# Attention denominators by way of DRAM, both value sums in one PSUM bank, and three banks for the scores

## The chip, the cores and the metric

The kernel runs on one core of one Trainium2 chip. The metric is the device time of one execution in microseconds (us), as a median over runs. The core has five engines that work side by side and wait for each other only by semaphores: TensorE (PE in the rows; PEld is its loading of stationary operands, which runs beside the matmuls), VectorE (DVE), ScalarE (ACT), GpSimd (POOL) and SyncE (SP), which here issues nearly all DMAs. TensorE writes to PSUM, a memory of 128 partitions with eight banks of 512 fp32 columns each.

## The reference, cut to what matters

A decoder layer works on x of 4 sequences, 512 tokens and 256 channels: a Mamba block, then causal attention plus attention to a context of 1024 tokens, then a feed-forward part with eight experts. The change lies in the attention:

```python
scale = np.float32(1.0 / np.sqrt(D))            # T = 512, TC = 1024, H = 16 heads of D = 16
q, k, v = heads(x @ Wq + bq), heads(x @ Wk + bk), heads(x @ Wv + bv)
att = where(causal, einsum('bhqd,bhkd->bhqk', q, k) * scale, -inf)
y = einsum('bhqk,bhkd->bhqd', softmax(att), v)
qc, kc, vc = heads(x @ Wcq + bcq), heads(ctx @ Wck + bck), heads(ctx @ Wcv + bcv)
attc = einsum('bhqd,bhkd->bhqk', qc, kc) * scale
y = y + einsum('bhqk,bhkd->bhqd', softmax(attc), vc)
x = x + y_as_rows @ Wp + bp
```

Each softmax has its own denominator, so for each head two sums over the keys are divided by two denominators and then added.

## The kernel before

One program handles the sequences b = 0 to 3 one after the other. For each, a block holds the stages `attend(b)` (attention of sequence b), `entry(b + 1)` (the end of b's attention, its normalisation and routing, mixed with the input projections of sequence b + 1) and `scan(b + 1)` (the Mamba scan). Every stage has one program for each engine, written out by hand; an engine runs its program strictly in order and waits by semaphores. In the last block the experts follow instead of a scan.

**Attention.** The 16 heads go in NG = 4 groups g of HG = 4 heads. A group has STEPS = 12 steps k: four causal ones (k = 0 to 3, 128 keys each, against the 512, 384, 256 and 128 queries that may see them) and eight context ones (k = 4 to 11, 128 keys each against 512 queries). In a step TensorE makes for each head h a tile of scores (`scores`, bf16), keys on partitions, ScalarE takes its exponential into `probs` (L1778), GpSimd cuts the causal diagonal (`masks`, L1498), and TensorE adds values times probabilities to the sums (`values(g, k)`, fp32, four heads side by side in 32 rows each). `values` of step k - 1 stands behind the scores of step k. The values have a column of ones, so row HD = 16 of each head's 32 rows holds its denominator.

**PSUM.** Banks 0 to 3 are two slots for the maxima, 4 and 5 the ring of score tiles (tile n waits until tile n - 2 is read), 6 holds the context sums, 7 the causal ones. The softmax subtracts true maxima: while group g is worked on, TensorE also makes the scores of group g + 1 as 24 jobs (`max_job`; 8 causal, 16 context, two matmuls or more each) and VectorE reduces them (L1813, L1809). The maxima are turned (`max_rows_out`, L1604), split into bf16 parts on VectorE (`negated_parts`, L1825 to L1830) and loaded by SyncE. `JOBS_AT` says how many jobs stand in each step: two per step while groups 1 and 2 are worked on, none in group 3, a mixed list in group 0. In a step with two jobs the order on TensorE is scores of heads 0 and 1, a job, scores of heads 2 and 3, a job, values; jobs that must wait for a turn stand behind the values.

**Denominators.** ScalarE copies bank 7 into `Y2` behind step 9 (L1761) and bank 6 into `Y1` behind the next group's step 0 (L1753). In the next group's step 1 TensorE spreads the denominator rows over all 128 partitions with a matmul by the 0-1 matrix `den_sel` (`denominators`, two fp32 matmuls of 512 columns in two ring slots), ScalarE copies the two results (L1767), and GpSimd and VectorE form (Y1 * d2 + Y2 * d1) / (d1 * d2): product on GpSimd (L1526), reciprocal on VectorE (L1835, or L1158 for group 3), three more multiplications and an addition on GpSimd, the last of them (L1536) into `YT[g]`. For group 3 this tail lies between the last attention step and `project`, the product with Wp, in `entry`: there TensorE first turns the next sequence's rows (`to_columns`), makes half of its input projection and then `project`; in the last block `project` follows at once.

## Time and profile before

| what | us |
|---|---|
| time, median of 3 runs (1931.35 to 1934.1) | 1931.47 |
| the profiled execution | 1937.27 |
| its span, first to last instruction | 1935.5 |
| TensorE busy in it | 1519.7 (79%) |
| VectorE busy | 1356.8 (70%) |
| ScalarE busy | 852.4 (44%) |
| GpSimd busy | 716.3 (37%) |
| mean DMA rate | 76 GB/s |
| TensorE's line L166 (nearly all matmuls), share of the chain that ended last | 16% |

The granted TensorE clock has a mean of 0.917 of full speed. Busy shares are means over stages of different kinds: in the scan VectorE is the busiest, in the attention TensorE. So they say little by themselves, and the stages have to be read one by one. The four attentions are alike: the copies of the context sums stand at 294.0, 335.4, 376.7 and 409.2 us for b = 0, and the same distances (41.3 to 41.4, 41.3 to 41.4 and 32.5 us) return for b = 1, 2 and 3. "L166" is a helper that records almost every matmul, so those are told apart by their tiles.

### The profile page before, as it was taken

How to read it: one execution, taken by the hardware profiler on the slowest of the kernel's cores; microseconds unless marked ns; L12 is line 12 of the kernel's file. 1: busy time of each engine (PE TensorE's matmuls, PEld its weight loads, DVE VectorE, ACT ScalarE, POOL GpSimd, SP SyncE). 2: the span in 40 equal slices, each digit the busy share in tenths (PEclk: the TensorE clock that was granted, in tenths of full speed). 3: DMA queues.
4: the chain of work that ended last, by engine and by line, in shares of the span. 5: the costliest groups of instructions: out<-in, count | busy, mean ns of one | idle time of the engine just before them, and what ended most of it. 6: DMA issues, size and time to landing. Idle time of an engine off the chain costs nothing. (4 is left out here: it accounts for less than half of the span.)

```text
span 1935.5 us, 19324 instructions
## 1 busy us (share of the span) xinstructions
PE 1519.7 (79%) x6456; PEld 726.0 (38%) x6456; DVE 1356.8 (70%) x2009; ACT 852.4 (44%) x1618; POOL 716.3 (37%) x678
## 2 busy tenths in 40 slices
PE   5697789883987798884977888845677998669995
PEld 2354322231554222142544222322232221458874
DVE  5998587658995777479995876579977684434334
ACT  3543346654543356644433466544333567212211
POOL 2564332322864412226653322227644222222221
PEclk9799889996999799987999799978998899779998
DMA  4930441003002530012004420021014300247754
GB/s 134 341 105 24 112 91 42 1 1 118 20 1 70 137 62 1 1 51 85 3 1 120 107 42 2 1 88 45 1 40 125 73 10 1 66 129 247 239 171 132
DMA packets 123843, 147.17 MB, mean 76 GB/s; under 512 B 18725, under 2 KB 106542, under 8 KB 121696
## 3 DMA queue, kind: packets, MB, share of 16 engines
q1 hardware_dynamic: 120000, 137.27, 24.4%
q0 software_dynamic: 3744, 8.66, 1.2%
q8 instruction: 51, 0.84, 0.2%
q14 instruction: 48, 0.39, 0.1%
HBM read 96.53 MB, written 50.79 MB: 76 GB/s over the span
## 5 line engine op out<-in xcount | busy, mean ns | idle before, releaser
L166 PE MATMUL PS<-arena 128*32 128x512 f32 (+10 forms) x4150 | 862.8, 451 | 117.6 <-ACT arena L1778 30.1
L166 PEld LDWEIGHTS PS<-arena 128*32 128x32 f32 (+3 forms) x4150 | 363.9, 128 | 598.3 <-ACT arena L1778 269.7
L1778 ACT ACTIVATE arena<-PS 128x512 f32<-128x512 f32 (+3 forms) x768 | 375.3, 541 | 271.0 <-PE PS L166 269.1
L1353 POOL TENSOR_TENSOR arena<-arena 128x1024 f32<-128x1024 f32 x128 | 305.1, 2385 | 239.1 <-DVE arena L1379 139.8
L1809 DVE TENSOR_REDUCE maxs<-PS 128x1 f32<-128x1024 f32 x256 | 301.3, 1216 | 53.6 <-PE PS L166 53.3
L1379 DVE TENSOR_TENSOR_SCAN arena<-PS,arena 128x1024 f32<-128x1024 f32 x128 | 292.1, 2282 | 6.1 <-ACT PS L1328 6.1
L1328 ACT ACTIVATE PS<-arena,A_neg 128x511 f32<-128x511 f32 x256 | 165.9, 681 | 240.3 <-DVE arena L1379 191.0
L166 PE MATMUL PS<-arena,ident 128*128 128x512 f32 (+1 forms) x560 | 259.8, 590 | 5.4 <-DVE arena L1388 5.4
L1498 POOL TENSOR_SCALAR_AFFINE_SELECT arena<-arena 128x128 f32<-128x128 f32 x256 | 73.7, 300 | 324.4 <-ACT arena L1778 320.4
L1388 DVE TENSOR_TENSOR arena<-arena,PS 128x1024 f32<-128x1024 f32 x128 | 156.2, 1220 | 6.9 <-PE PS L166 2.8
L1813 DVE TENSOR_REDUCE maxs<-PS 128x1 f32<-128x512 f32 (+3 forms) x256 | 107.9, 481 | 62.8 <-PE PS L166 62.0
L166 PE MATMUL PS<-bc,bc_sel 96*128 96x512 bf16 x128 | 52.1, 407 | 121.0 <-DVE arena L1388 114.4
L166 PEld LDWEIGHTS PS<-arena,ident 128*128 128x128 f32 x560 | 109.4, 199 | 91.9 <-issue 74.5
L530 POOL DMA_INDIRECT picked_rows<-arena x46 | 45.3, 985 | 142.7 <-DVE arena L708 82.7
L166 PEld LDWEIGHTS PS<-bc,bc_sel 96*128 96x128 bf16 x128 | 12.5, 97 | 174.6 <-DVE arena L1388 163.6
L1487 POOL TENSOR_TENSOR arena<-arena 128x512 bf16<-128x512 f32 x40 | 46.0, 1155 | 81.2 <-ACT arena L1724 81.2
L1801 DVE SCALAR_TENSOR_TENSOR arena<-PS,bqk,arena 128x512 f32<-128x512 f32 x40 | 29.5, 747 | 63.9 <-ACT arena L1719 63.9
L1719 ACT ACTIVATE arena<-PS,bqk 128x512 bf16<-128x512 f32 x40 | 26.9, 683 | 94.5 <-PEq L173 52.7
L617 ACT ACTIVATE arena<-PS,arena 128x256 f32<-128x256 f32 x60 | 25.2, 471 | 91.7 <-PE PS L166 91.7
L1526 POOL TENSOR_TENSOR arena<-xn 128x512 f32<-128x512 f32 x16 | 20.3, 1266 | 114.9 <-ACT xn L1767 114.9
L166 PE MATMUL PS<-xT,in_w 128*128 128x512 f32 x128 | 59.3, 619 | 3.1 <-DVE xT L1154 3.1
L1835 DVE RECIPROCAL arena<-arena 128x512 f32<-128x512 f32 x12 | 40.1, 3344 | 28.7 <-POOL arena L1526 28.7
(260 smaller groups left out, 1632.1 us busy)
## 6 DMA issues: line engine op xcount, KB each, us to landing
arena<-in_ew SPq DMA_DIRECT2D x46, 512.0 KB, 4.6
arena<-stack_parts SPq DMA_DIRECT2D x288, 64.0 KB, 2.2
rows_in<-nil SPq DMA_DIRECT2D x16, 1088.0 KB, 12.5
arena<-b_rows SPq DMA_DIRECT2D x16, 1024.0 KB, 7.6
stack_parts<-arena SPq DMA_DIRECT2D x40, 384.0 KB, 2.5
arena<-stack_parts SPq DMA_DIRECT2D x96, 128.0 KB, 4.1
arena<-rows_in SPq DMA_DIRECT2D x23, 272.0 KB, 5.0
arena<-picked_rows SPq DMA_DIRECT2D x16, 256.0 KB, 3.5
```

The costliest lines, as they stand in the source:

```text
L166: return nc.tensor.matmul(o, l, r, start=start, stop=stop)
L530: nc.gpsimd.indirect_dma_start(picked_rows, bass.IndirectOffsetOnAxis(ap=row_id[i % NIB][:, r:r + 1].bitcast(I32), axis=0), eo[i % NEB][:, ...
L1328: last = nc.scalar.activation(decay(i)[:, k, 1:T], delta[:, 2 * kh + k, 1:T], ACT.Exp, scale=A_neg[:, 2 * kh + k, n:n + 1])
L1353: nc.gpsimd.tensor_tensor(b_sb[i % 2], u[:, 2 * kh:2 * kh + 2, :], Brow[:, n, :].unsqueeze(1).to_broadcast([P, 2, T]), ALU.mult).then_inc( ...
L1379: nc.vector.tensor_tensor_scan(h_sb[i % 2].rearrange(flat), decay(i).rearrange(flat), b_sb[i % 2].rearrange(flat), 0.0, ALU.mult, ALU.add)\
L1388: nc.vector.tensor_tensor(g_sb[i % 2], h_sb[i % 2], bank(6).unsqueeze(1).to_broadcast([P, 2, T]), ALU.mult).then_inc(S["g_done"], 1)
L1487: nc.gpsimd.tensor_tensor(pt[i % NPT][:, 2, :], r_sb[i % 2], pt[i % NPT][:, 1, :], ALU.subtract)\
L1498: nc.gpsimd.affine_select(out=own, in_=own, compare_op=ALU.is_ge, fill=0.0, base=0, pattern=[[1, P]], channel_multiplier=-1).then_inc(S["m ...
L1778: nc.scalar.activation(probs[(HG * s + h) % NPR][:, 0:N], bank(4 + n % 2)[:, 0:N], ACT.Exp, scale=HD ** -0.5).then_inc(S["ring_read"], 1)
L1809: last = nc.vector.reduce_max(maxs[:, g % 2, CONTEXT, h * TT + r:h * TT + r + 1], PS[:, 2 * s:2 * s + 2, :].rearrange("p a n -> p (a n)"), ...
L1813: last = nc.vector.reduce_max(maxs[:, g % 2, CAUSAL, h * TT + q:h * TT + q + 1], bank(2 * s + c_)[:, 0:(q + 1) * P], AXX)
L1835: nc.vector.reciprocal(R2, R1).then_inc(S["norm_ready"], 1)
```

## The change

The tail of each group is done in another way, and the PSUM banks are given out anew.

- Both sums of a group use bank 6, causal first, then context. `copy_causal` moves from behind step 9 to behind step 4, and `values` of step 0 and step 4 wait for the copy of the sum before them. Bank 7 joins the ring of score tiles, which has three banks now.
- `Y1`, `Y2` become two pairs of buffers `YS`, taken in turn by the groups.
- For groups 0 to 2 the `den_sel` matmuls, ScalarE's copies of them, and the reciprocal of 128x512 are gone. SyncE gathers the denominator rows into `den_c` (32 partitions of 128), VectorE inverts that in place, SyncE writes it to `dens` in DRAM and reads it back, each head's row repeated over 32 partitions, into `den_sb`. GpSimd then does two multiplications and an addition. SyncE's loads of group 3's heads, of 24 DMAs, stand between the gather and the write for group 0; the loads of the rows of maxima for group g + 2 stand behind the read.
- For group 3 TensorE multiplies the sums, as stationary operand, with four columns of `den_sel` (`turned_sums`: eight fp32 matmuls of 4 columns), VectorE inverts 32 columns and repeats each 32 times (`last_sums`), TensorE turns that into two banks (`spread_sums`: eight fp32 matmuls of 128 columns), and VectorE multiplies and adds (`last_heads`).

ScalarE's order around the end of group 1. L1761 and L1753 (before), L1799 and L1791 (after) are the copies of the causal and the context sums, L1767 the copies of the spread denominators, L1778 and L1809 the exponentials. Before:

```order
L1778 ACTIVATE arena<-PS 128x512 x24
L1761 ACTIVATE arena<-PS 128x512
L1778 ACTIVATE arena<-PS 128x512 x12
L1753 ACTIVATE arena<-PS 128x512
L1778 ACTIVATE arena<-PS 128x384 x4
L1767 ACTIVATE xn<-PS 128x512 x2
L1778 ACTIVATE arena<-PS 128x256 x4
```

After:

```order
L1809 ACTIVATE arena<-PS 128x512 x4
L1799 ACTIVATE arena<-PS 128x512
L1809 ACTIVATE arena<-PS 128x512 x32
L1791 ACTIVATE arena<-PS 128x512
L1809 ACTIVATE arena<-PS 128x384 x4
L1809 ACTIVATE arena<-PS 128x256 x4
```

The causal copy moved from behind 24 context exponentials to behind four; the two denominator copies are gone.

TensorE's order from the last values of group 3 on (`32x512` is a head's part of `values`), before:

```order
L166 MATMUL PS<-arena 32x512 x8
L166 MATMUL PS<-arena,den_sel 128x512 x2
L452 MATMUL PS<-ident,arena 128x128 x8
L166 MATMUL PS<-xT,in_w 128x512 x8
L166 MATMUL PS<-wp,arena 128x256 x16
```

After:

```order
L170 MATMUL PS<-arena 32x512 x8
L170 MATMUL PS<-den_sel,arena 128x4 x8
L456 MATMUL PS<-ident,arena 128x128 x8
L170 MATMUL PS<-ident,xn 128x128 x8
L170 MATMUL PS<-xT,in_w 128x512 x8
L170 MATMUL PS<-wp,arena 128x256 x16
```

Sixteen matmuls in two places stand where two stood; the second eight are ahead of the input projection.

VectorE's order at the same place (the first row of each is its copy in the turning of x, the last the convolution), before:

```order
L1154 COPY xT<-PS 128x512
L1155 MEMSET arena 128x4x3
L1158 RECIPROCAL arena<-arena 128x512
L1053 TENSOR_SCALAR arena<-arena,conv_w,conv_b 128x512
L1056 SCALAR_TENSOR_TENSOR arena<-arena,conv_w 128x512 x3
```

After:

```order
L1173 RECIPROCAL den_t<-PS 128x32
L1175 COPY xn<-den_t 128x1024
L1193 COPY xT<-PS 128x512
L1194 MEMSET arena 128x4x3
L1182 TENSOR_TENSOR arena<-arena,PS 128x512
L1183 TENSOR_TENSOR arena<-arena,PS 128x512
L1184 TENSOR_TENSOR arena<-arena 128x512
L1074 TENSOR_SCALAR arena<-arena,conv_w,conv_b 128x512
```

A short reciprocal and a copy now stand ahead of the copy of x, and three multiplications and additions take the place of the long reciprocal.

The diff, cut to its core:

```diff
@@ -50,6 +50,7 @@
...
     picked_rows = nc.dram_tensor("picked_rows", (NOWHERE, DM), F32).ap()
+    dens = nc.dram_tensor("dens", (2, HG, T), F32).ap()
@@ -125,6 +126,9 @@
...
         mrest = sb("mrest", [HG * TT, P])
+        den_c = sb("den_c", [2 * HG * TT, P])
+        den_t = sb("den_t", [P, 2 * TT * HG])
+        den_wide = xn[:].rearrange("p (i a) n -> p i (a n)", i=2)
@@ -355,7 +359,7 @@
...
         yt_end = used[0]
-        Y1, Y2, R1, R2 = ar(T), ar(T), ar(T), ar(T)
+        YS = [(ar(T), ar(T)) for _ in range(2)]
@@ -756,10 +760,7 @@
...
         def ring(g, k, h):
-            return HG * (STEPS * g + k) + h + 2 * max(g - 1, 0) + (2 if g >= 1 and k >= 2 else 0)
-
-        def ring_den(g, i):
-            return HG * STEPS * (g + 1) + 2 * g + i + (2 * HG if g + 1 < NG else 0)
+            return HG * (STEPS * g + k) + h
@@ -827,6 +828,22 @@
...
             def tensor(pe):
+                def turned_sums():
+                    pe.wait_ge(S["pv_copied"], 2 * NG)
+                    for i, y in enumerate(YS[(NG - 1) % 2]):
+                        for t in range(TT):
+                            last = mm(bank(5)[:, (i * TT + t) * HG:(i * TT + t + 1) * HG], y[:, tok(t)],
+                                      den_sel[:, 0:P:32], i + t == 0, i + t == TT)
+                    last.then_inc(S["turned_mm"], 1)
+
+                def spread_sums():
+                    pe.wait_ge(S["den_ready"], NG)
+                    for i in range(2):
+                        for t in range(TT):
+                            last = mm(bank(6 + i)[:, tok(t)], den_wide[:, i, tok(t)],
+                                      ident[:], True, True)
+                    last.then_inc(S["turned_mm"], 1)
+
@@ -889,7 +906,11 @@
...

+                if ends:
+                    pe.wait_ge(S["ring_read"], HG * STEPS * NG)
+                    turned_sums()
                 if not begins:
+                    spread_sums()
@@ -898,9 +919,9 @@
...
                     to_columns(pe, xnE, TT * ends, 0)
+                    if ends:
+                        spread_sums()
                     pe.wait_ge(S["xT_ready"], 2 + 2 * ends)
-                    if ends:
-                        pe.wait_ge(S["ring_read"], ring_den(NG - 1, 1) + 1)
@@ -1147,15 +1168,32 @@
...

+                def last_sums():
+                    dve.wait_ge(S["turned_mm"], 1)
+                    fed(nc.vector.reciprocal(den_t[:], bank(5)[:, 0:2 * TT * HG]))
+                    dve.wait_ge(S["y_ready"], NG - 1)
+                    nc.vector.tensor_copy(den_wide.rearrange("p i (c n) -> p (i c) n", n=32),
+                                          den_t[:].unsqueeze(2).to_broadcast([P, 2 * TT * HG, 32]))\
+                        .then_inc(S["den_ready"], 1)
+
+                def last_heads():
+                    dve.wait_ge(S["turned_mm"], 2)
+                    y = YS[(NG - 1) % 2]
+                    fed(nc.vector.tensor_tensor(y[0], y[0], bank(6), ALU.mult))
+                    fed(nc.vector.tensor_tensor(y[1], y[1], bank(7), ALU.mult))
+                    nc.vector.tensor_tensor(YT[NG - 1], y[0], y[1], ALU.add).then_inc(S["y_ready"], 1)
+
...
                     normalise(dve, link, x_sb, xnE)
+                if ends:
+                    last_sums()
+                if begins:
...
                 if ends:
-                    dve.wait_ge(S["den_ready"], NG)
-                    nc.vector.reciprocal(R2, R1).then_inc(S["norm_ready"], 1)
+                    last_heads()
@@ -1393,6 +1431,11 @@
...
             CAUSAL, CONTEXT = 0, 1
+            RING = (4, 5, 7)
+
+            def ring_bank(n):
+                return bank(RING[n % len(RING)])
+
@@ -1469,12 +1512,24 @@
...
                 load_max_rows(1, CONTEXT)
-                sp.wait_ge(S["pv_mm"], STEPS)
-                for x in range(4):
-                    load_heads(3, x)
-                for g in range(2, NG):
-                    for side in range(2):
-                        load_max_rows(g, side)
+                for g in range(NG - 1):
+                    sp.wait_ge(S["pv_copied"], 2 * (g + 1))
+                    for i, y in enumerate(YS[g % 2]):
+                        sp.dma_start(den_c[i * HG * TT:(i + 1) * HG * TT, :], y[HD:P:32, :])\
+                            .then_inc(S["dens_out"], 16)
+                    if g == 0:
+                        for x in range(4):
+                            load_heads(3, x)
+                    sp.wait_ge(S["den_ready"], g + 1)
+                    sp.dma_start(dens.rearrange("i h (q p) -> (i h q) p", p=P), den_c[:]).then_inc(S["dens_kept"], 16)
+                    sp.wait_ge(S["dens_kept"], 16 * (g + 1))
+                    sp.wait_ge(S["y_ready"], g)
+                    for i in range(2):
+                        sp.dma_start(den_sb[:, i, :], dens[i].unsqueeze(1).to_broadcast([HG, 32, T]))\
+                            .then_inc(S["dens_in"], 16)
+                    if g + 2 < NG:
+                        load_max_rows(g + 2, CAUSAL)
+                        load_max_rows(g + 2, CONTEXT)
@@ -1518,22 +1573,14 @@
...
                 pool.wait_ge(S["ones_ready"], 2 * NPAR)
-                for g in range(NG):
-                    if g + 1 < NG:
-                        masks(g + 1, 0)
-                        masks(g + 1, 1)
-                    pool.wait_ge(S["ring_read"], ring_den(g, 1) + 1)
-                    nc.gpsimd.tensor_tensor(R1, den_sb[:, 0, :], den_sb[:, 1, :], ALU.mult)\
-                        .then_inc(S["den_ready"], 1)
-                    if g + 1 < NG:
-                        masks(g + 1, 2)
-                    nc.gpsimd.tensor_tensor(Y1, Y1, den_sb[:, 1, :], ALU.mult)
-                    if g + 1 < NG:
-                        masks(g + 1, 3)
-                    link(nc.gpsimd.tensor_tensor(Y2, Y2, den_sb[:, 0, :], ALU.mult))
-                    link(nc.gpsimd.tensor_tensor(Y1, Y1, Y2, ALU.add))
-                    pool.wait_ge(S["norm_ready"], g + 1)
-                    nc.gpsimd.tensor_tensor(YT[g], Y1, R2, ALU.mult).then_inc(S["y_ready"], 1)
+                for g in range(NG - 1):
+                    for k in range(TT):
+                        masks(g + 1, k)
+                    pool.wait_ge(S["dens_in"], 2 * 16 * (g + 1))
+                    y = YS[g % 2]
+                    nc.gpsimd.tensor_tensor(y[0], y[0], den_sb[:, 0, :], ALU.mult)
+                    link(nc.gpsimd.tensor_tensor(y[1], y[1], den_sb[:, 1, :], ALU.mult))
+                    nc.gpsimd.tensor_tensor(YT[g], y[0], y[1], ALU.add).then_inc(S["y_ready"], 1)
@@ -1608,9 +1655,9 @@
...
                         n = ring(g, k, h)
-                        if n >= 2:
-                            pe.wait_ge(S["ring_read"], n - 1)
-                        o = bank(4 + n % 2)
+                        if n >= len(RING):
+                            pe.wait_ge(S["ring_read"], n - len(RING) + 1)
+                        o = ring_bank(n)
@@ -1618,21 +1665,15 @@
...

-                def denominators(g):
-                    pe.wait_ge(S["pv_copied"], 2 * (g + 1))
-                    for i, y in enumerate((Y1, Y2)):
-                        pe.wait_ge(S["ring_read"], ring_den(g, i) - 1)
-                        mm(bank(4 + ring_den(g, i) % 2), den_sel[:], y, True, True).then_inc(S["ring_mm"], 1)
-
...
                     if k == 0 and g >= 1:
-                        pe.wait_ge(S["pv_copied"], 2 * g - 1)
-                    if k == TT and g >= 1:
                         pe.wait_ge(S["pv_copied"], 2 * g)
+                    if k == TT:
+                        pe.wait_ge(S["pv_copied"], 2 * g + 1)
@@ -1640,7 +1681,7 @@
...
                         else:
-                            last = mm(bank(7)[rows, k * P:T], V[:, k, HG * g + h, :],
+                            last = mm(bank(6)[rows, k * P:T], V[:, k, HG * g + h, :],
@@ -1698,8 +1739,6 @@
...
                             max_job(g + 1, i)
-                        if k == 1 and g >= 1:
-                            denominators(g - 1)
@@ -1750,22 +1788,15 @@
...
                     act.wait_ge(S["pv_mm"], STEPS * (g + 1))
-                    nc.scalar.activation(Y1, bank(6), ACT.Copy).then_inc(S["pv_copied"], 1)
+                    nc.scalar.activation(YS[g % 2][0], bank(6), ACT.Copy).then_inc(S["pv_copied"], 1)
...
                         all_stored(act)
-                    else:
-                        act.wait_ge(S["y_ready"], g)
+                    if g >= 2:
+                        act.wait_ge(S["y_ready"], g - 1)
                     act.wait_ge(S["pv_mm"], STEPS * g + TT)
-                    nc.scalar.activation(Y2, bank(7), ACT.Copy).then_inc(S["pv_copied"], 1)
-
-                def copy_denominators(g):
-                    for i in range(2):
-                        n = ring_den(g, i)
-                        act.wait_ge(S["ring_mm"], n + 1)
-                        nc.scalar.activation(den_sb[:, i, :], bank(4 + n % 2), ACT.Copy)\
-                            .then_inc(S["ring_read"], 1)
+                    nc.scalar.activation(YS[g % 2][1], bank(6), ACT.Copy).then_inc(S["pv_copied"], 1)
@@ -1775,16 +1806,13 @@
...
                         act.wait_ge(S["ring_mm"], n + 1)
-                        nc.scalar.activation(probs[(HG * s + h) % NPR][:, 0:N], bank(4 + n % 2)[:, 0:N], ACT.Exp,
+                        nc.scalar.activation(probs[(HG * s + h) % NPR][:, 0:N], ring_bank(n)[:, 0:N], ACT.Exp,
...
                         copy_context(g - 1)
-                    if g >= 1 and k == 1:
-                        copy_denominators(g - 1)
-                    if k == STEPS - 3:
+                    if k == TT:
...
                 copy_context(NG - 1)
-                copy_denominators(NG - 1)
@@ -1831,8 +1859,10 @@
...
                 def invert(g):
-                    dve.wait_ge(S["den_ready"], g + 1)
-                    nc.vector.reciprocal(R2, R1).then_inc(S["norm_ready"], 1)
+                    dve.wait_ge(S["dens_out"], 2 * 16 * (g + 1))
+                    if g:
+                        dve.wait_ge(S["dens_kept"], 16 * g)
+                    nc.vector.reciprocal(den_c[:], den_c[:]).then_inc(S["den_ready"], 1)
@@ -1858,11 +1888,10 @@
...
                         negated_parts(g + 1, CAUSAL)
-                        maxima(g + 1, range(KJOBS, KJOBS + 4))
...
                     if g + 1 < NG:
-                        maxima(g + 1, range(KJOBS + 4, JOBS))
+                        maxima(g + 1, range(KJOBS, JOBS))
...
                     for k in range(KM):
```

## Rows read from the trace of the kernel before

**Rows 1.** Stretches (us): busy PE, PEld, DVE, ACT, POOL; granted clock; DMA share, GB/s.
```profile
294.00:335.36 41.36, 37.35 (x215) 11.04 (x214) 31.91 (x41) 25.73 (x52) 10.78 (x21) 1.00 0.22 49
376.71:409.18 32.47, 25.73 (x144) 5.98 (x142) 10.14 (x26) 23.44 (x48) 9.48 (x17) 1.00 0.01 1
```
**Rows 2.** Timeline of ScalarE: start, duration, instruction, idle time before and its releaser.
```profile
291.43 2.17 ACT L1778 ACTIVATE arena<-PS 128x512 f32<-128x512 f32 x4 [1.22 <-PE PS L166]
...
304.64 2.17 ACT L1778 ACTIVATE arena<-PS 128x512 f32<-128x512 f32 x4 [1.07 <-PE PS L166]
...
322.63 2.17 ACT L1778 ACTIVATE arena<-PS 128x512 f32<-128x512 f32 x4 [1.21 <-PE PS L166]
...
326.01 2.17 ACT L1778 ACTIVATE arena<-PS 128x512 f32<-128x512 f32 x4 [0.72 <-PE PS L166]
```
**Rows 3.** Timeline of TensorE's weight loads, one context step with two maxima jobs.
```profile
318.76 0.55 PEld L166 LDWEIGHTS PS<-arena 99*128 99x128 bf16 x4 [0.84 <-ACT arena L1778]
319.90 0.10 PEld L166 LDWEIGHTS PS<-arena 99*128 99x128 bf16 x1 [0.59 <-ACT arena L1778]
320.39 0.33 PEld L166 LDWEIGHTS PS<-arena 99*128 99x128 bf16 x3 [0.39 <-ACT arena L1778]
```
**Rows 4.** Timeline of VectorE in the same group, behind the turn of the maxima.
```profile
307.10 4.62 DVE L1809 TENSOR_REDUCE maxs<-PS 128x1 f32<-128x1024 f32 x4
311.63 3.34 DVE L1835 RECIPROCAL arena<-arena 128x512 f32<-128x512 f32 x1
```
**Rows 5.** Timeline, a context step of group 3: ScalarE and TensorE's weight loads.
```profile
402.79 2.16 ACT L1778 ACTIVATE arena<-PS 128x512 f32<-128x512 f32 x4 [0.29 <-PE PS L166]
403.44 0.10 PEld L166 LDWEIGHTS PS<-arena 99*128 99x128 bf16 x1 [1.02 <-ACT arena L1778]
...
403.93 0.10 PEld L166 LDWEIGHTS PS<-arena 99*128 99x128 bf16 x1 [0.39 <-ACT arena L1778]
...
405.24 0.11 PEld L166 LDWEIGHTS PS<-arena 99*128 99x128 bf16 x2 [0.84 <-ACT arena L1778]
```
**Rows 6.** Timeline, the end of the attention of b = 0.
```profile
409.18 0.60 ACT L1753 ACTIVATE arena<-PS 128x512 f32<-128x512 f32 x1 [1.29 <-PE PS L166]
...
409.83 1.98 PE L166 MATMUL PS<-arena,den_sel 128*128 128x512 f32 x4 [0.72 <-ACT arena L1753]
...
413.47 7.13 PE L166 MATMUL PS<-xT,in_w 128*128 128x512 f32 x16 [0.78 <-DVE xT L1154]
...
417.17 0.70 DVE L1053 TENSOR_SCALAR arena<-arena,conv_w,conv_b 128x512 f32<-128x512 f32 x1
```
**Rows 7.** Timeline, the same place for b = 3.
```profile
1650.10 0.60 ACT L1753 ACTIVATE arena<-PS 128x512 f32<-128x512 f32 x1 [1.29 <-PE PS L166]
...
1659.88 9.56 PE L166 MATMUL PS<-wp,arena 128*128 128x256 f32 x32 [7.15 <-POOL arena L1536]
```
**Rows 8.** Timeline of TensorE in the scan.
```profile
103.72 0.38 PE L166 MATMUL PS<-bc,bc_sel 96*128 96x512 bf16 x1
103.94 2.32 PE L166 MATMUL PS<-arena,ident 128*128 128x512 f32 x8
106.10 1.24 PE L166 MATMUL PS<-arena 128*128 128x256 f32 x5
```
**Rows 9.** Groups of instructions by form: busy us, mean ns of one, idle before.
```profile
L1388 DVE TENSOR_TENSOR arena<-arena,PS 128x1024 f32<-128x1024 f32 x128 | 156.2, 1220 | 6.9 <-PE PS L166 2.8
...
L1526 POOL TENSOR_TENSOR arena<-xn 128x512 f32<-128x512 f32 x16 | 20.3, 1266 | 114.9 <-ACT xn L1767 114.9
L1146 DVE TENSOR_TENSOR arena<-arena 128x512 f32<-128x512 f32 x16 | 19.5, 1218 | 1.9 <-ACT arena L988 1.9
```
**Rows 10.** DMA issues on the page: count, KB each, median us to landing.
```profile
arena<-stack_parts SPq DMA_DIRECT2D x288, 64.0 KB, 2.2
...
arena<-b_rows SPq DMA_DIRECT2D x16, 1024.0 KB, 7.6
```
**Rows 11.** Timeline of SyncE: its queue issues the loads of group 3's heads.
```profile
294.70 11.56 SPq L1430 DMA_DIRECT2D arena<-stack_parts  x24
```

5 lines of the change are left out of this document (2 added, 3 removed).

## The prediction

> **What bounds the kernel now.** I read three views: busy time by stretch, to see which engine fills a group of the attention; the timelines of single steps there, to see what TensorE waits for; and the timeline of the attention's end, where the change adds a serial chain. A group of the middle (from one context copy to the next) takes 41.36 us with TensorE busy for 37.35, VectorE for 31.91 and ScalarE for 25.73; group 3, with no maxima to make, takes 32.47 us with TensorE at 25.73 and ScalarE at 23.44 [rows 1]. So no engine is full, and TensorE is the nearest to it. The bracket [0.59 <-ACT] in the steady context step tells what it lacks: the load for head 2's scores stands at 319.90 until ScalarE has freed a bank, that for head 3 at 320.39 until it has freed the next [rows 3]. Group 3 repeats it: 403.44 and 403.93, each after an exponential [rows 5]. With two banks, TensorE's order ties it to ScalarE twice in every step. ScalarE itself is not full: four exponentials take 2.17 us, and it then stands still for 1.21 us until TensorE is through with job, values and next score [rows 2]. The bound is this round trip, and the scores' ring sets it.
>
> **The third bank.** Head 2's scores now need the bank that head 3 of the step before used, free for long. Head 3's need head 0's bank, the release on which head 2 waited before. So head 3, and all behind it, moves from 320.39 to 319.90, by 0.49 us; in group 3 from 403.93 to 403.44, again 0.49 [rows 3, 5]. Does TensorE get there in time? From 318.76 it has two scores, a job of two matmuls and head 2's scores ahead of head 3's, five bf16 matmuls of 512 columns at 0.22 us (103.72 to 103.94) [rows 8]: 1.10 us, to 319.86. It just fits. ScalarE's 2.17 us fit into the new step of 3.38 - 0.49 = 2.89 us (322.63 to 326.01 is 3.38 now) [rows 2], and so do two maxima of 4.62 / 4 = 1.16 us [rows 4]. Where it applies the gain is 0.49 us a step:
> - Groups 1 and 2, eight context steps each. Behind the turn VectorE is late, so one or two steps stay longer, but the reciprocal of 3.34 us between the maxima [rows 4] becomes one of 128 columns, 3.34 / 4 = 0.84 us, ahead of them. I take 4.0 us a group, about 8 x 0.49.
> - The four causal steps have tiles of 512 down to 128 columns and exponentials to match, so the gain shrinks with them; I take 1.1 us a group.
> - Group 0: its first steps hold three or four jobs and are paced by VectorE; the last four gain 2.0 us.
> - Group 3: 8 x 0.49 = 3.9 us and 1.1 for the causal steps, less 0.9 below.
>
> **Denominators of groups 0 to 2.** TensorE loses two fp32 products of 512 columns, four passes. Four passes and four of 128 columns take 106.10 - 103.94 = 2.16 us; at a rate by columns that is 0.43 and 0.11 us each [rows 8], so 1.72 us go. It also waited there for ScalarE, as at the end of group 3 (0.72) [rows 6]; I take 2.0 us in all, and the first four steps, 13.21 us long (291.43 to 304.64) [rows 2], get shorter by 3.1. Five GpSimd operations of 1.27 us [rows 9] become three. GpSimd has 10.78 us of work in a group of 41.36 [rows 1], so that gives nothing.
>
> What comes in is a chain by way of SyncE. From the copy in step 0: a gather, a reciprocal, a write, a read of two times 256 KB, three GpSimd operations. 64 KB land in 2.2 us, and one of four loads of 1024 KB in 7.6 us [rows 10], so the small transfers are 2 us each and the read 2 to 8 us. Behind the first gather SyncE issues 24 loads in 11.56 us [rows 11]; the write queues behind them. Worst: 0.6 + 2 + 11.6 + 2 + 8 + 3.8 = 28 us, and the new group has about 34; the buffers that it frees are wanted only a group later. Queued behind SyncE's waits are the rows of maxima for group g + 2, wanted 34 us after they are made. VectorE waits for the gather at step 4, some 10 us into the group, when it has landed. All hidden, cost 0.
>
> **One bank for both sums.** `values` of step 0 wait for the context copy, `values` of step 4 for the causal one. Both stand behind a whole step's scores, and head 3's scores themselves need an exponential that ScalarE makes after the copy. So the copy is done when `values` ask, and its price is its 0.6 us on ScalarE, where that is short. In steps of 2.89 us with 2.17 of exponentials it is hidden (before, too, it cut the idle time from 1.21 to 0.72) [rows 2]. In group 3 a step is 2.94 - 0.49 = 2.45 us against 2.16 [rows 5]: 0.3 shows. There step 4, behind the short step 3, is also paced by ScalarE and does not gain its 0.49. I take 0.9 together; the bounds are 0 and, if a copy lay bare, 0.6 + 2.17 = 2.8 us for each of 32 copies.
>
> **Sum of an attention.** Groups 1 and 2: 4.0 + 3.1 = 7.1 each. Group 3: 3.9 + 3.1 - 0.9 = 6.1. Group 0: 2.0. Together 22.3 us; times four, 89.2.
>
> **The end, b = 0 to 2.** Time runs from ScalarE's copy at 409.18 [rows 6]. Now the input projection begins at 4.29. After: the copy ends at 0.6; `turned_sums` are 16 passes of 4 columns behind fp32 weight loads. The trace has no such pass: nearest is the fp32 pass of 128 columns at 0.11 [rows 8]; below it is some 0.03, above a 128-column load and a pass one after the other, 0.3. I take 0.09, 1.5 us, to 2.2. VectorE's reciprocal of 32 columns is 3.34 / 16 = 0.2 [rows 4], its copy of 1024 columns 0.6 to 1.2 (1.22 for a product of that size) [rows 9]: to 3.9 with semaphores. The turning of x, and its copies, lie beside. `spread_sums` are 16 passes of 128 columns, 1.8 us, to 5.7. The projection begins 1.4 us later than now, and `project` with it. VectorE's two products from PSUM (half of 1.22 each) and one sum in SBUF (1.22) [rows 9] end near 8.3, against 8.0 when the convolution starts now [rows 6], and the long reciprocal and its wait are gone. So + 1.4 us, three times + 4.2. Bounds: 0.5 and, with 0.3 us for all 32 passes, 6.5 each.
>
> **The end, b = 3.** Now `project` begins 1659.88 - 1650.10 = 9.78 us after the copy [rows 7]. After: 8.3, so - 1.5. TensorE stood still for 7.15 us, and `project` then took 9.56 us for 32 passes of 256 columns, where 0.22 each would be 6.9. With shorter gaps some of that may come back. I take - 2 in all (0 to - 4).
>
> **Sum.** - 89.2 + 4.2 - 2 = - 87 us. The profiled execution took 1937.27 us, with 1.8 outside its span; it becomes 1850.3. The median of the runs lies 5.8 below the profiled one: 1844.5, so 1845.
>
> **A rule that speaks against it.** In the read back from DRAM each of four heads' rows is repeated 32 times, and the outer dimension of the source is 4. The trace shows no such read; its load of repeated rows has the partitions outermost and lands in 7.6 us for 1024 KB [rows 10]. The Trainium skill, DMA: Bandwidth & Descriptors, Rules for kernel authors, says that an outer dimension below 16 confines a DMA to so many of the 16 engines, and names a leading broadcast as the case. By that rule the two reads would share four engines; the sum would be the same as long as rival 2's condition is not met.
>
> **The rivals.**
> 1. *VectorE takes the place of the ring.* It has 31.91 us of work in a group [rows 1], less 2.5 for the reciprocal, and the new group has 34. Its maxima follow TensorE's jobs through two slots, so a late one stops TensorE, and the catching up behind the turn may take four steps and not two. For it: after the turn VectorE runs 4.62 and 3.34 us without a gap [rows 4]. Against: per step 2.3 us against 2.89. Then about half of the gain of 28 steps x 4 is lost, 0.25 x 112 = 28 us: 1873.
> 2. *The DRAM chain is late.* If the read runs at a quarter of the rate, 256 KB take 4 x 256 / 1024 x 5.6 = 5.6 us beyond the fixed 2, two of them 13 us. In group 3 the chain of group 2 is then 3.2 + 0.6 + 2 + 0.9 + 2 + 13 + 3.8 = 25.5 us, against 26 for the group and 3 more until VectorE needs it: hidden. It decides from 29 us on; at twice the read it costs 9 us in each attention: 1880. This is the skill's rule above, taken to one or two engines.
> 3. *The waits on ScalarE are not what they seem.* If each step is held by something that the brackets do not name, only the den_sel matmuls go: 3 x 2 x 4 = 24 us, + 2 at the ends: 1910.
> 4. *Slower: the shared bank lays the copies bare.* If each handover of bank 6 stops TensorE, that is 32 times up to 2.8 us, 90 us; it decides from 87 / 32 = 2.7 us a handover. Against: a step's scores stand between. It would give 1845 + 90 = 1935.
>
> **Chances.** The forecast, 1830 to 1865: 0.62. Rival 1: 0.16. Rival 2: 0.06. Rival 3: 0.06. Rival 4: 0.03, with ends of 6.5 us each and less gain in the ring. Faster than 1830: 0.07. Range 1830 to 1882, which holds the forecast, rival 1 mostly and rival 2. About 0.2% (4 us) is what a measurement of this kernel can tell from no change. Faster by more: 0.95; within: 0.02; slower: 0.03.
>
> **What would show it.** In the changed profile: context steps of 2.9 us in groups 1 and 2 and 2.45 in group 3, with one wait for ScalarE per step instead of two; middle groups of 34 us, group 3 near 26; the projection starting about 5.7 us after the last copy. Rival 1 would show VectorE without gaps and TensorE waiting for L1837; rival 2 VectorE's copy waiting for GpSimd; rival 4 `values` waiting for ScalarE's copies. The prediction fails first if the steps do not shrink by 0.49 us.

## The result, and the profile after the change

The changed kernel takes 1850.99 us (median of 4 runs, 1846.17 to 1856.06) beside 1932.78 us for the kernel before (4 runs, 1931.35 to 1935.59): a ratio of 0.9575, 95% interval 0.9544 to 0.9607. The prediction of 1845 us with a range of 1830 to 1882 held. The profiled execution took 1853.68 us, where the prediction's own sum had 1850.3. Timed once more in a later set the ratio was 0.957 [0.9546, 0.9594].

Two stretches by busy time, the first from one context copy to the next, the second group 3 (columns: length, then busy time with the number of instructions for PE, PEld, DVE, ACT and POOL, then granted clock, DMA share, GB/s). They answer to [rows 1]:

```profile
289.56:323.99 34.43, 33.11 (x211) 10.19 (x210) 28.22 (x41) 23.62 (x50) 8.25 (x19) 1.00 0.33 75
358.42:384.85 26.43, 22.23 (x140) 5.18 (x138) 6.00 (x26) 21.13 (x46) 7.38 (x16) 1.00 0.07 23
```

A middle group is 6.9 us shorter, group 3 is 6.0 us shorter, and TensorE now works for 33.1 of 34.4 us in a middle group, where it worked for 37.35 of 41.36. The same lengths return in all four attentions (one middle group of b = 2 is 34.71 us long). What a step looks like now, in ScalarE's timeline (start, duration, instruction, idle time before and its releaser), first groups 1 and 2, then group 3; they answer to [rows 2, 5]:

```profile
304.54 2.06 ACT L1809 ACTIVATE arena<-PS 128x512 f32<-128x512 f32 x4 [1.20 <-PE PS L170]
307.43 2.07 ACT L1809 ACTIVATE arena<-PS 128x512 f32<-128x512 f32 x4 [0.83 <-PE PS L170]
...
364.41 2.06 ACT L1809 ACTIVATE arena<-PS 128x512 f32<-128x512 f32 x4 [0.67 <-PE PS L170]
366.34 0.63 ACT L1799 ACTIVATE arena<-PS 128x512 f32<-128x512 f32 x1
366.81 2.12 ACT L1809 ACTIVATE arena<-PS 128x512 f32<-128x512 f32 x4
369.32 2.06 ACT L1809 ACTIVATE arena<-PS 128x512 f32<-128x512 f32 x4 [0.39 <-PE PS L170]
371.77 2.07 ACT L1809 ACTIVATE arena<-PS 128x512 f32<-128x512 f32 x4 [0.39 <-PE PS L170]
```

The steps are 307.43 - 304.54 = 2.89 us and 371.77 - 369.32 = 2.45 us. The weight loads of the same step show what is left of TensorE's waits, to be read against [rows 3]:

```profile
306.94 0.76 PEld L170 LDWEIGHTS PS<-arena 99*128 99x128 bf16 x5 [0.84 <-ACT arena L1809]
308.08 0.33 PEld L170 LDWEIGHTS PS<-arena 99*128 99x128 bf16 x3 [0.38 <-ACT arena L1809]
```

The scores of heads 0 and 1, the job and the scores of head 2 run through (five loads in one row), and the next load waits for ScalarE; before, head 2 and head 3 each waited.

The end of the attention of b = 0, TensorE and VectorE, to be read against [rows 6] (the passes of fp32 count twice, as x16):

```profile
385.59 1.92 PE L170 MATMUL PS<-den_sel,arena 128*128 128x4 f32 x16 [0.81 <-ACT arena L1791]
387.37 1.07 PE L456 MATMUL PS<-ident,arena 128*128 128x128 f32 x8
388.69 2.05 PE L170 MATMUL PS<-ident,xn 128*128 128x128 f32 x16 [0.25 <-DVE xn L1175]
390.58 3.60 PE L170 MATMUL PS<-xT,in_w 128*128 128x512 f32 x8
...
387.55 0.36 DVE L1173 RECIPROCAL den_t<-PS 128x32 f32<-128x32 f32 x1 [18.89 <-PE PS L170]
387.94 0.69 DVE L1175 COPY xn<-den_t 128x1024 f32<-128x1024 f32 x1
```

The projection begins 390.58 - 384.85 = 5.73 us behind the last copy (4.29 before). The same row of `spread_sums` is longer behind b = 1 (3.35 us) and b = 2 (3.65 us), and the stretch around it has a lower granted clock; here is b = 1, and the stretch behind b = 0 and 1:

```profile
778.32 3.35 PE L170 MATMUL PS<-ident,xn 128*128 128x128 f32 x16 [0.25 <-DVE xn L1175]
```

```profile
386.90:390.60 3.70, 3.45 (x31) 3.21 (x31) 1.67 (x4) 0.60 (x1) 0.00 (x0) 1.00 0.00 0
776.90:781.40 4.50, 4.25 (x27) 4.02 (x27) 1.67 (x4) 0.60 (x1) 0.00 (x0) 0.71 0.00 0
```

Last, the chain through DRAM, in SyncE's and GpSimd's timelines of the first middle group:

```profile
290.87 1.25 SPq L1518 DMA_DIRECT2D den_c<-arena  x2
292.17 11.46 SPq L1473 DMA_DIRECT2D arena<-stack_parts  x24
303.67 0.42 SPq L1524 DMA_DIRECT2D dens<-den_c  x1
308.91 1.16 SPq L1528 DMA_DIRECT2D xn<-dens  x2
...
316.81 1.27 POOL L1581 TENSOR_TENSOR arena<-arena,xn 128x512 f32<-128x512 f32 x1 [19.64 <-DMA xn<-dens]
...
319.38 1.27 POOL L1583 TENSOR_TENSOR arena<-arena 128x512 f32<-128x512 f32 x1
322.56 0.29 POOL L1553 TENSOR_SCALAR_AFFINE_SELECT arena<-arena 128x128 f32<-128x128 f32 x1 [1.90 <-ACT arena L1809]
```

GpSimd's third operation ends at 320.65, 31.1 us behind the copy at 289.56. The row below it is the first mask of the next group, which GpSimd takes up 1.90 us later. That bracket is all the slack that the chain has on GpSimd here.

Where the 83.6 us of the two profiled executions came from (us over all four sequences). "Tiles" are ScalarE's first reads of the query and key projections ahead of the attention (L1719 before, L1757 after); the other cuts are its copies of the context sums:

| stretch | predicted | measured |
|---|---|---|
| start of the program to the first tile of b = 0 | 0 | -1.1 |
| last tile to the first copy: group 0, with step 0 of group 1 | -8.0 | -14.0 |
| groups 1 and 2 | -56.8 | -55.0 |
| group 3 | -24.4 | -24.2 |
| last copy to the next block's first tile (the end and the scan), b = 0 to 2 | +4.2 | +7.4 |
| first to last tile | 0 | +2.6 |
| behind the last attention | -2.0 | +0.75 |
| sum | -87.0 | -83.6 |

### The profile page after: what moved, and what is told of

Same layout as the page of the kernel before. It is cut to its first block and busy times, and to the rows that moved or that the text cites. A ratio compares the mean times of both kernels' runs of the same rounds, so it can differ in the third digit from the quotient of the medians.

```text
span 1851.9 us, 19445 instructions
## 1 busy us (share of the span) xinstructions
PE 1474.7 (80%) x6520; PEld 730.4 (39%) x6520; DVE 1306.0 (71%) x2025; ACT 818.5 (44%) x1586; POOL 660.6 (36%) x634
## 5 line engine op out<-in xcount | busy, mean ns | idle before, releaser
L170 PE MATMUL PS<-arena 128*32 128x512 f32 (+10 forms) x4150 | 830.2, 449 | 84.4 <-DVE maxs L1837 22.0
L1809 ACT ACTIVATE arena<-PS 128x512 f32<-128x512 f32 (+3 forms) x768 | 361.6, 549 | 225.5 <-PE PS L170 224.4
L1581 POOL TENSOR_TENSOR arena<-arena,xn 128x512 f32<-128x512 f32 x12 | 15.3, 1274 | 163.1 <-DMA xn<-dens 163.1
L1757 ACT ACTIVATE arena<-PS,bqk 128x512 bf16<-128x512 f32 x40 | 26.9, 682 | 97.4 <-PEq L177 52.8
L646 DVE CAST arena<-arena 128x2 int32<-128x2 f32 x23 | 4.1, 176 | 78.3 <-PE PS L547 68.9
```

The lines of the kernel that those rows point to most:

```text
L170: return nc.tensor.matmul(o, l, r, start=start, stop=stop)
L1809: nc.scalar.activation(probs[(HG * s + h) % NPR][:, 0:N], ring_bank(n)[:, 0:N], ACT.Exp, scale=HD ** -0.5).then_inc(S["ring_read"], 1)
```

## Experiments

All edits are to the changed kernel. "Middle group" is the distance between the context copies of groups 0 and 1, and of 1 and 2.

**1. The third bank, taken away.**

```diff
-            RING = (4, 5, 7)
+            RING = (4, 5)
```

> The changed kernel with a ring of two banks (4 and 5); bank 7 lies idle, everything else is as changed. Theory (the third bank carries most of the gain, 0.49 us a step): context steps back at 3.38 us in groups 1 and 2 and at 2.94 in group 3; middle groups of about 38.6 to 39.3 us (34.43 with three banks), group 3 of about 31 (26.43); 17 us more per attention, about 1920 us in all, which would leave some 13 us of the 82 to the denominators alone. Rival (the two waits on ScalarE in each step are not what holds it; only the den_sel matmuls that went did): middle groups stay within 1 us of 34.4 and the time within 10 us of 1851.

Measured: 1918.65 us (4 runs), ratio to the kernel before 0.9929 [0.9901, 0.9957]. Middle groups of 38.38 us, group 3 of 31.78 us (b = 0 and 3), 30.70 (b = 1) and 30.47 (b = 2). The difference within group 3 goes with the granted clock, b = 0 first, then b = 1:

```profile
370.51:402.29 31.78, 25.29 (x140) 5.37 (x138) 6.11 (x26) 22.25 (x46) 7.16 (x15) 0.95 0.06 19
778.25:808.95 30.70, 23.77 (x140) 5.30 (x138) 6.20 (x26) 22.25 (x46) 7.15 (x15) 1.00 0.06 19
```

TensorE's weight loads in a context step:

```profile
308.72 0.55 PEld L170 LDWEIGHTS PS<-arena 99*128 99x128 bf16 x4 [0.84 <-ACT arena L1809]
309.86 0.10 PEld L170 LDWEIGHTS PS<-arena 99*128 99x128 bf16 x1 [0.59 <-ACT arena L1809]
310.35 0.33 PEld L170 LDWEIGHTS PS<-arena 99*128 99x128 bf16 x3 [0.39 <-ACT arena L1809]
```

Both waits of [rows 3] are back, 0.49 us apart (309.86, 310.35), and the step is 3.38 us again. So the ring carries 1918.65 - 1850.99 = 67.7 of the 82 us; the prediction's terms for it are 5.1 + 5.1 + 5.0 + 2.0 = 17.2 in each attention, 69 in all. Rival 3 falls.

**2. Banks of their own for the two sums, with a ring of two.** It differs from experiment 1 in the sharing alone.

```diff
-            RING = (4, 5, 7)
+            RING = (4, 5)
...
-                    if k == 0 and g >= 1:
-                        pe.wait_ge(S["pv_copied"], 2 * g)
-                    if k == TT:
-                        pe.wait_ge(S["pv_copied"], 2 * g + 1)
+                    if k == 0 and g >= 1:
+                        pe.wait_ge(S["pv_copied"], 2 * g - 1)
+                    if k == TT and g >= 1:
+                        pe.wait_ge(S["pv_copied"], 2 * g)
...
-                            last = mm(bank(6)[rows, k * P:T], V[:, k, HG * g + h, :],
+                            last = mm(bank(7)[rows, k * P:T], V[:, k, HG * g + h, :],
...
-                    nc.scalar.activation(YS[g % 2][1], bank(6), ACT.Copy).then_inc(S["pv_copied"], 1)
+                    nc.scalar.activation(YS[g % 2][1], bank(7), ACT.Copy).then_inc(S["pv_copied"], 1)
```

> A ring of two banks again, and bank 7 now takes the causal sums, so that causal and context sums have banks of their own as in the kernel before; `values` wait for the copy of a group earlier. It differs from the run with two banks in the sharing alone, and from the kernel before in the way of the denominators alone. Theory (the handover of the shared bank is hidden behind a step's scores): the same time as the run with two banks within 4 us, about 1920. Rival (each of the 32 handovers stops TensorE by 0.3 us or more): at least 10 us faster than the run with two banks. Against the kernel before, the theory gives what the denominators' way saves by itself: 3 x 3.1 us less 0.5 x 3 per attention at most, 5 to 20 us in all.

Measured: 1921.08 us (5 runs), ratio 0.993 [0.9904, 0.9956]. Middle groups of 38.38 us, the same to the hundredth as with the shared bank; group 3 of 31.79 at b = 0 and 31.78 at b = 3, as in experiment 1. At b = 1 and 2 it is 31.95 and 33.29 us long, 1.25 and 2.8 us longer than there, at a granted clock of 0.95 and 0.85 where experiment 1 has 1.00; so banks of their own are nowhere faster. The handovers cost nothing that can be measured, with two banks in the ring. With three, in group 3, where ScalarE is short, the two steps around the causal copy take 369.32 - 364.41 = 4.91 us, twice the 2.45 of a step without it. Rival 4 falls.

The two runs also split a middle group: 41.34 to 38.38 by the other way of the denominators (2.96 us), 38.38 to 34.43 by the ring (3.95 us). The whole kernel shows less of the first part: experiments 1 and 2 are 12 to 15 us faster than the kernel before, where 8 x 2.96 is 23.7. The stretches between the attentions, which hold the changed ends, took back 10 us of it (the first two rows of the table under experiment 8).

**3. The chain through DRAM, left out.**

```diff
...
-                    for i, y in enumerate(YS[g % 2]):
-                        sp.dma_start(den_c[i * HG * TT:(i + 1) * HG * TT, :], y[HD:P:32, :])\
-                            .then_inc(S["dens_out"], 16)
...
-                    sp.wait_ge(S["den_ready"], g + 1)
-                    sp.dma_start(dens.rearrange("i h (q p) -> (i h q) p", p=P), den_c[:]).then_inc(S["dens_kept"], 16)
...
-                    if g >= 1:
-                        invert(g - 1)
...
-                    pool.wait_ge(S["dens_in"], 2 * 16 * (g + 1))
+                    pool.wait_ge(S["pv_copied"], 2 * (g + 1))
```

> The changed kernel without the chain through DRAM in groups 0 to 2: the gather, VectorE's inversion, the write and the read are left out (30 DMAs and 3 reciprocals of 0.93 us per attention), and GpSimd multiplies by whatever lies in den_sb as soon as the sums are copied. The denominators of these groups are therefore not computed; the last group's are. Theory (chain fully hidden): the same time within 4 us, 1851; at most the standstill of 1 us behind the turn in the middle groups shrinks by VectorE's 0.93 us, 8 times, so a gain of 0 to 7 us. Rival (the chain delays TensorE through SyncE's queue, DMA traffic or GpSimd's masks): faster by more than 10 us.

Measured: 1862.5 us (4 runs), ratio 0.9626 [0.9597, 0.9655]: work was left out and the kernel became 11.5 us slower. Neither theory had that sign. Middle groups of 35.35 and 36.82 us. VectorE behind the turn in the second, and GpSimd at the same time:

```profile
336.04 0.84 DVE L1847 CAST mparts<-mrest 16x128 bf16<-16x128 f32 x1
336.92 1.38 DVE L1848 TENSOR_TENSOR mparts<-mrest,mparts 16x128 bf16<-16x128 f32 x1
338.23 4.69 DVE L1827 TENSOR_REDUCE maxs<-PS 128x1 f32<-128x1024 f32 x4
...
335.54 1.27 POOL L1572 TENSOR_TENSOR arena<-arena,xn 128x512 f32<-128x512 f32 x1
336.89 1.26 POOL L1573 TENSOR_TENSOR arena<-arena 128x512 f32<-128x512 f32 x1
```

VectorE's two operations end at 336.88 and 338.30, each just behind the end of one of GpSimd's (336.81, 338.15). In the changed kernel the same two take 0.21 and 0.28 us, because the chain holds GpSimd's work back until 316.81. The maxima behind them start when GpSimd is through. That such reads of PSUM are not held up is seen in the changed kernel, where two of them take 2.36 us, their usual 1.2 us each, beside the operation of GpSimd at 316.81:

```profile
316.70 2.36 DVE L1837 TENSOR_REDUCE maxs<-PS 128x1 f32<-128x1024 f32 x2 [0.54 <-PE PS L170]
```

The 1.73 us lost, less the 0.93 us of the inversion that is gone, are 0.8 of the 0.92 us by which the first middle group is longer; in the second TensorE's clock fell as well (0.95 over the group), behind 2.26 us in which it waited for the maxima. Over the four attentions the groups are 13.3 us longer by the trace.

**4. The same, with GpSimd's work held back.**

```diff
                     pool.wait_ge(S["pv_copied"], 2 * (g + 1))
+                    pool.wait_ge(S["ring_read"], HG * (STEPS * (g + 1) + 10))
```

> As the run without the chain through DRAM (the denominators of groups 0 to 2 are not computed, their gather, inversion, write and read left out), but GpSimd's three operations on a group's sums wait until the tenth step of the next group, when the changed kernel has them too (316 us). In the run without the chain they began right behind the masks, at 334.3, while VectorE's CAST and TENSOR_TENSOR on mparts took 0.84 and 1.38 us (0.21 and 0.28 in the changed kernel). Theory (GpSimd's SBUF work and VectorE's SBUF-to-SBUF work hold each other up, and that made the run without the chain 11 us slower): those two are back at 0.21 and 0.28 us, middle groups are 33.5 to 34.4 us long, and the time is 1842 to 1851. Rival (the chain's absence shifts something else, such as the loads of maxima): middle groups stay at 35.3 and 36.8 us, the time near 1862.

Measured: 1851.99 us (4 runs), ratio 0.9574 [0.9554, 0.9594]; middle groups of 34.03 us. GpSimd's first operation begins at 316.00, and VectorE's two rows are back:

```profile
299.83 0.21 DVE L1848 CAST mparts<-mrest 16x128 bf16<-16x128 f32 x1
300.08 0.28 DVE L1849 TENSOR_TENSOR mparts<-mrest,mparts 16x128 bf16<-16x128 f32 x1
```

One wait more, and the kernel is 10.5 us faster; by the traces the eight middle groups together are 289.02 us long in experiment 3 and 272.55 here. So it was the meeting of the two engines, and what followed from it. The chain itself (DMAs, SyncE's queue, the inversion of 0.93 us) costs 34.43 - 34.03 = 0.4 us in a middle group and no more.

**5. The chain made longer: the read made four times, and twice.**

```diff
-                    for i in range(2):
-                        sp.dma_start(den_sb[:, i, :], dens[i].unsqueeze(1).to_broadcast([HG, 32, T]))\
-                            .then_inc(S["dens_in"], 16)
+                    for r in range(4):
+                        for i in range(2):
+                            sp.dma_start(den_sb[:, i, :], dens[i].unsqueeze(1).to_broadcast([HG, 32, T]))\
+                                .then_inc(S["dens_in"], 16)
+                        sp.wait_ge(S["dens_in"], 2 * 16 * (4 * g + r + 1))
```

> The changed kernel with the read back from DRAM made four times, each pair of DMAs waited for by SyncE before the next is issued: the read takes about 4 x 7.9 = 32 us instead of 7.9, so the chain is some 24 us longer. Theory (the chain ends 8.3 us before group 3 does: 376.5 against 384.85, and GpSimd's product is wanted by VectorE's copy 3 us behind that, so 11 us of slack): the end of the attention, between the last copy and the input projection, becomes 12 to 15 us longer, 4 x 13 = 52 us, and more where the middle groups' masks and buffers are late too; the time is 1895 to 1960. Rival (the slack is larger than read, GpSimd's work being wanted only later): less than 10 us more in all.

Measured with four reads: 2056.87 us (4 runs), 206 us more and not 52. By stretches at b = 0: the first middle group 57.04 us (+22.6), the second 50.20 (+15.8), group 3 26.43 (unchanged), and VectorE's copy at the end came 14.99 us behind the last context copy in place of 3.09 (+11.9). Only this last term had been expected with a number. For the others I took GpSimd's queue: the masks of the next group stand behind its three operations, and `values` of step 0 wait for the masks. The slack on that path was read off the changed trace, and the read made twice (the same edit with 2 for 4) was to put it to the test:

> The changed kernel with the read back from DRAM made twice, so that the chain is some 8 us longer. With the read made four times the chain was 23 us longer, and the groups between context copies became 22.6 and 15.8 us longer and the end 11.9. Theory (the chain is wanted first where the next group's masks queue behind GpSimd's three operations; its slack in the changed trace is 322.56 - 320.65 = 1.9 us in the first middle group, 356.99 - 347.87 = 9.1 in the second, and 387.94 - 376.50 = 11.4 at the end): the first middle group becomes 6 to 8 us longer, 40.5 to 42.5 us, the second stays at 34.4 to 35.5, group 3 at 26.4, the end unchanged; 24 to 32 us in all, 1875 to 1883. Rival (the chain is wanted only at the end of a group or later, as the prediction took it): all groups unchanged, 1851.

Measured: 1886.46 us (one time). The first middle group is 42.64, 42.37, 41.69 and 42.14 us long, the second 34.42 (34.70 at b = 2, as unchanged), group 3 27.64 for b = 0 to 2 and 26.44 for b = 3. Columns as in the first fence:

```profile
291.66:334.30 42.64, 34.42 (x211) 10.44 (x210) 28.31 (x41) 23.70 (x51) 8.54 (x20) 0.92 0.30 73
334.30:368.72 34.42, 33.11 (x211) 10.18 (x210) 28.21 (x41) 23.72 (x51) 7.98 (x18) 1.00 0.09 33
368.72:396.36 27.64, 23.73 (x140) 5.28 (x138) 6.01 (x26) 21.17 (x47) 7.38 (x16) 0.94 0.12 41
```

The middle groups are about as long as expected, but another wait ended last. In the first middle group SyncE, GpSimd and TensorE's weight loads have:

```profile
327.46 7.36 SPq L1481 DMA_DIRECT2D arena<-mparts  x6
...
330.08 1.26 POOL L1585 TENSOR_TENSOR arena<-arena 128x512 f32<-128x512 f32 x1
...
330.49 0.14 PEld L170 LDWEIGHTS PS<-arena 99*128 99x128 bf16 x2 [7.83 <-issue]
...
331.87 0.29 POOL L1555 TENSOR_SCALAR_AFFINE_SELECT arena<-arena 128x128 f32<-128x128 f32 x1 [0.53 <-ACT arena L1811]
```

TensorE stands still for 7.83 us ahead of the first scores of group 2, not ahead of `values`. It goes on at 330.49, before GpSimd's third operation ends (331.34), and the first mask then waits for ScalarE. What the scores of step 0 wait for in the program is the rows of maxima of their group. SyncE loads these behind the read, and the edit also makes it wait until the last read has landed. TensorE goes on 3.03 us behind the first of these loads (327.46); with four reads it is 3.02 and 3.08 us (339.32 to 342.34, and 389.47 to 392.55). In the second middle group of this run the loads begin at 361.23 and the scores are due at 366.12: nothing is lost. So the edit's cost in the middle groups came by way of SyncE's queue. GpSimd's way would have cost nearly as much: its third operation ends 39.68 us behind the context copy in place of 31.09, 8.6 us later for a slack of 1.9. That slack is read from the changed trace; no run tests it by itself. In the changed kernel the same loads begin at 310.11, and the scores of group 2 at 321.40, so that way has some 8 us of slack.

Group 3 is 1.2 us longer for b = 0 to 2 at a granted clock of 0.94, which the expectation did not have; that is 3.6 of the 35 us, where 24 to 32 had been expected in all.

**6. The read with 32 repeats outermost.**

```diff
-                        sp.dma_start(den_sb[:, i, :], dens[i].unsqueeze(1).to_broadcast([HG, 32, T]))\
-                            .then_inc(S["dens_in"], 16)
+                        for h in range(HG):
+                            sp.dma_start(den_sb[32 * h:32 * h + 32, i, :], dens[i, h].partition_broadcast(32))\
+                                .then_inc(S["dens_in"], 16)
```

> The read back from DRAM as eight DMAs of one head each, whose outermost dimension is 32 repeats, in place of two with an outermost dimension of 4. In the changed kernel the two moved at some 100 GB/s with a DMA share of 0.20 to 0.25, and GpSimd began 7.9 us after the first was issued. Rival (the rate is set by the DRAM side or the packets of 2 KB, whatever the order): rate and share as before, GpSimd 8 us or more behind. In either case the time is within 5 us of 1851, since the chain is hidden.

Measured: 1847.63 us (one time; nothing follows from it alone). GpSimd begins 314.95 - 309.80 = 5.15 us behind the first issue in place of 316.81 - 308.91 = 7.90. A stretch in the middle of the read, first of the changed kernel, then of this one (the last two columns are DMA share and GB/s):

```profile
311.00:316.00 5.00, 5.00 (x30) 1.33 (x30) 4.46 (x4) 3.45 (x7) 0.00 (x0) 1.00 0.27 100
```

```profile
311.00:315.00 4.00, 4.00 (x22) 1.15 (x22) 2.93 (x4) 2.78 (x6) 0.05 (x1) 1.00 0.40 127
```

A share of 0.27 is 4.3 of 16 engines, with the small loads of the maxima among it. The Trainium skill's rule that the prediction weighed (DMA: Bandwidth & Descriptors, Rules for kernel authors: an outer dimension of 4 keeps a DMA on 4 of the 16 engines) agrees with it. With eight DMAs the share is 0.40, below the 0.5 expected, and SyncE takes 3.56 us to issue them; that issuing now sets the pace is likely, but was not tried. What the two DMAs cost is 2.75 us of a chain that lies hidden: middle groups are 34.42 us long with eight DMAs too.

**7. `turned_sums` with passes of 128 columns.**

```diff
-                            last = mm(bank(5)[:, (i * TT + t) * HG:(i * TT + t + 1) * HG], y[:, tok(t)],
-                                      den_sel[:, 0:P:32], i + t == 0, i + t == TT)
+                            last = mm(bank(4 + i)[:, tok(t)], y[:, tok(t)], den_sel[:], True, True)
...
-                    fed(nc.vector.reciprocal(den_t[:], bank(5)[:, 0:2 * TT * HG]))
+                    fed(nc.vector.reciprocal(den_t[:].rearrange("p (i c) -> p i c", i=2), PS[:, 4:6, 0:T:32]))
```

> `turned_sums` stream all 128 columns of den_sel (8 fp32 products of 128 columns, into banks 4 and 5) in place of 4 of them, and VectorE's reciprocal reads every 32nd column of the result; all else is as changed. In the changed kernel the granted clock over `spread_sums` was 1.00 behind b = 0, but 0.60 and 0.54 behind b = 1 and 2, where they took 3.3 us in place of 2.0. Theory (the passes of 4 columns count as rest for the clock): with the wide ones `spread_sums` are granted 1.00 behind every b, take 2.0 us, and the projection begins 5.8 us behind the last copy in all of them, so 2.6 us less in all, or nothing measurable but visible in the trace. Rival (the clock falls from the standstill while VectorE inverts and copies, or from what lies ahead): the clock over `spread_sums` stays below 0.7 in b = 1 and 2.

Measured: 1844.67 us (4 runs), ratio 0.9542 [0.9523, 0.9562], which overlaps the changed kernel's interval. The mean of 0.71 behind b = 1 lies between the two levels of the clock, half (1.2 GHz) and full (2.4 GHz). The same stretch here, and the rows in it:

```profile
776.30:780.10 3.80, 3.50 (x31) 3.26 (x31) 1.67 (x4) 0.60 (x1) 0.00 (x0) 1.00 0.00 0
```

```profile
775.04 2.02 PE L170 MATMUL PS<-den_sel,arena 128*128 128x128 f32 x16 [0.81 <-ACT arena L1790]
...
778.24 2.05 PE L170 MATMUL PS<-ident,xn 128*128 128x128 f32 x16 [0.30 <-DVE xn L1174]
```

Thirty-two times the columns cost 2.02 us in place of 1.92, the clock stays at 1.00 there behind b = 1 and 2, and `spread_sums` take 2.05 us behind all four, so 1.3, 1.6 and 0.8 us less behind b = 1, 2 and 3. The other traces bear this out behind b = 3 alone: there `spread_sums` take 2.8 to 3.8 us in all ten with passes of 4 columns, and 2.05 us in all three with 128. Behind b = 0 to 2 the narrow passes alone do not explain the clock: experiments 3 and 6 have them too, and take 2.05 us each time, as experiment 7 does. So what lies ahead of them counts as well, and the gain there is not shown to be the wide passes' doing. Nor is it shown that the whole kernel is faster by them.

**8. The ends in another order** (the turning of x ahead of `turned_sums`, two products of the projection ahead of `spread_sums`, the first convolution ahead of `last_heads`).

```diff
                     to_columns(pe, xnE, TT * ends, 0)
                     if ends:
-                        spread_sums()
+                        pe.wait_ge(S["ring_read"], HG * STEPS * NG)
+                        turned_sums()
                     pe.wait_ge(S["xT_ready"], 2 + 2 * ends)
                     for m in range(2 * DT):
+                        if ends and m == 2:
+                            spread_sums()
...
                 if ends:
-                    last_heads()
+                    last_sums()
                 if begins:
                     conv(0)
+                if ends:
+                    last_heads()
```

> The changed kernel with the ends b = 0 to 2 in another order: the turning of x and its copy stand ahead of `turned_sums`, two products of the input projection (m = 0, 1) ahead of `spread_sums`, and VectorE makes the first convolution ahead of the last group's products. Theory (the projection waits for the serial chain of the last denominators only because it stands behind it): it begins 2 to 4.3 us behind the last copy in place of 5.73, and the ends get shorter by 1.3 to 2.9 us each: 4 to 9 us in all, 1842 to 1847. Rival (the end is set by VectorE's work on the heads and by `project`, whatever stands ahead of it): within 3 us of 1851.

Measured: 1849.47 us (5 runs), ratio 0.9566 [0.9549, 0.9582]: within 2 us of the changed kernel. That is the rival's time but not its reason, since the end itself did as meant:

```profile
386.60:397.00 10.40, 10.40 (x55) 7.05 (x54) 6.83 (x12) 2.98 (x5) 0.00 (x0) 1.00 0.01 2
```

```profile
389.12 3.68 PE L170 MATMUL PS<-xT,in_w 128*128 128x512 f32 x8
```

TensorE works without a gap, and the projection begins 2.52 us behind the last copy. `project` begins 11.26 us behind it for b = 0 to 2, in place of 12.60, 14.24 and 14.23, so the three ends are 7.3 us shorter. At the next attention 3.3 us are left of that. Lengths from the last context copy of b to the first of b + 1:

| version | b = 0 | b = 1 | b = 2 |
|---|---|---|---|
| before | 296.23 | 301.21 | 297.99 |
| 1, two banks | 299.20 | 305.67 | 300.39 |
| changed | 294.33 | 300.71 | 299.70 |
| changed, once more | 294.41 | 300.69 | 299.70 |
| 7, wide passes | 296.58 | 294.32 | 296.54 |
| 8, other order | 297.29 | 297.21 | 296.92 |
| 9, both | 297.26 | 297.80 | 296.39 |
| 10, all | 294.67 | 294.65 | 294.65 |

The pattern of the changed kernel returned to 0.1 us in a second profiled execution (1853.68 and 1853.54 us). Its other executions took 1846 to 1858 us, so it need not always return. It differs between b = 0 and b = 1 although the work is the same. What differs is the clock in places far from the edit. The ten us from 40 us behind the copy of b = 0 on, in the changed kernel and in version 9:

```profile
424.85:434.85 10.00, 8.26 (x26) 4.29 (x24) 6.78 (x14) 9.70 (x16) 0.00 (x0) 1.00 0.59 223
```

```profile
426.99:436.99 10.00, 10.00 (x23) 5.82 (x23) 6.13 (x11) 9.71 (x16) 0.00 (x0) 0.66 0.74 301
```

**9 and 10. Versions that put the edits together.** Version 9 is 7 and 8 together. Version 10 adds experiment 6 and moves the inversion behind six context maxima:

```diff
-                    if g >= 1:
-                        invert(g - 1)
                     if g + 1 < NG:
-                        maxima(g + 1, range(KJOBS, JOBS))
+                        maxima(g + 1, range(KJOBS, KJOBS + 6))
+                    if g >= 1:
+                        invert(g - 1)
+                    if g + 1 < NG:
+                        maxima(g + 1, range(KJOBS + 6, JOBS))
```

> Two edits together: `turned_sums` with passes of 128 columns (8 us of b = 0 to 3 at full clock in place of half) and the ends in the other order (projection begins 2.5 us behind the last copy in place of 5.7). Theory (the two gains add up, 1 to 2.6 us in the ends b = 0 to 2 and 1.5 us at b = 3 for the clock): 5 to 8 us faster than the changed kernel, ratio to it 0.9957 to 0.9973, about 1844. Rival (what the ends win is given back in the blocks between the attentions, whose length differs by up to 6 us from execution to execution with the granted clock): within 3 us of it.

> The version before it, and in the attention VectorE's inversion of the denominators behind the first six context maxima in place of ahead of them, and the read back from DRAM as eight DMAs with 32 repeats outermost (GpSimd began 5.2 us behind the first issue with these, 7.9 without), so that GpSimd's products are done at about 319 us, ahead of the masks at 322.6. Theory (VectorE's 0.93 us ahead of the maxima is what holds TensorE behind the turn: middle groups were 34.03 us long without the inversion and 34.43 with it): middle groups 34.0 to 34.1 us, 8 x 0.4 = 3.2 us less than the version before it, about 1841. Rival (the inversion costs the same wherever it stands, or the later chain runs into the masks of the next group): middle groups 34.4 or longer, no gain.

> The changed kernel as it is, timed beside the two versions of this set. Its ratio to the kernel before was 0.9575 [0.9544, 0.9607]. Theory (the ratio is steady from set to set): 0.955 to 0.960. Rival (sets differ by more than 0.3%, so that versions of different sets can't be told apart): outside of that.

Measured beside each other, 5 runs each: the changed kernel 1850.54 us, 0.957 [0.9546, 0.9594]; version 9 1849.63 us, 0.9568 [0.9553, 0.9582]; version 10 1838.19 us, 0.9506 [0.9492, 0.952]. Version 9 gained nothing. Version 10 beats both kernels. Its VectorE and its middle group:

```profile
303.90 2.36 DVE L1840 TENSOR_REDUCE maxs<-PS 128x1 f32<-128x1024 f32 x2 [0.41 <-PE PS L170]
306.18 0.93 DVE L1868 RECIPROCAL den_c<-den_c 32x128 f32<-32x128 f32 x1
```

```profile
288.73:322.76 34.03, 33.11 (x211) 10.19 (x210) 28.20 (x41) 23.63 (x51) 8.25 (x19) 1.00 0.34 76
```

The inversion now fills VectorE's gaps and the middle group is 34.03 us long, as it was without any inversion: 8 x 0.4 = 3.2 us, as expected. The order of the read is not the cause, since experiment 6 alone left 34.42. Most of the rest of the 11.4 us by which it beats version 9 lies between the attentions (the row of the table adds up to 891.45 us there and to 883.97 here, 7.5 less), in code that is the same in both; by the traces another 3 us lie ahead of the first copy. Between the attentions it goes with the granted clock: from 40 to 60 and from 60 to 80 us behind the last copy of b = 0 it is 0.65 and 0.50 in version 9, 0.75 and 0.56 in version 10. This was not designed; why the pattern of version 10 is the short one stays open.

## Why the prediction was right, point by point

The mechanism was right: some four fifths of the gain are the third bank's (experiment 1), at the price per step that was forecast. That the sum came within 3.5 us of the profiled time is partly luck. Group 0 and the start gave 7.1 us more than predicted, and groups 1 to 3, the ends, the tiles and the stretch behind the last attention gave 10.6 us less.

**What bounds the kernel** held. The brackets [0.59 <-ACT] and [0.39 <-ACT] of [rows 3] were the bound: with the third bank one of the two goes, and the step shrinks by 0.49 us, to 2.89 and 2.45, to the hundredth. "It just fits" held as well, since the loads in front of the second wait run through. Experiment 1 puts them back.

**The split between ring and denominators** was off inside a right sum. For a middle group the prediction had 5.1 us for the ring (4.0 and 1.1 for causal steps) and 2.0 for the denominators; the runs show 3.95 and 2.96. Of the 2.96, 2.00 lie in the first four steps, as predicted: from the last exponentials of a group to the first context ones it is 13.21 us before and 302.32 - 291.11 = 11.21 in experiment 1. The other 0.96 lie behind the turn, where the long reciprocal stood; the prediction named it, but had no term of its own for it. Of the ring's 3.95, 3.4 are seven times 0.49, 0.44 lie in the causal steps (1.1 predicted), and the first two context steps give 0.1. Behind the turn there still is one longer step: ScalarE starts at 304.54 behind a bracket of 1.20 where the next has 0.83. The inversion's share in what is lost there is 0.4 us (experiment 4 and version 10). In group 3, at a granted clock of 1.00, the denominators gave 1.8 to 2.0 us (32.47 to 30.70 and 30.47, experiment 1) and the ring 4.0 to 4.3.

**Group 0** was the term most off: - 2.0 us an attention was predicted, - 3.1 to - 4.0 measured. I had let only the last four steps with two jobs gain. The stretch measured also holds step 0 of group 1, and the steps with three jobs gained too: the context exponentials begin at 272.30, 275.76 and 278.78, steps of 3.46 and 3.02 us where the trace before has 3.81 and 3.38. Together with the 0.48 of step 0 that makes 3.2. The rest behind b = 1 and 2 was not looked into.

**"All hidden, cost 0"** was right to 0.4 us a middle group, but the chain had 1.9 us to spare on GpSimd and not the 6 us that the working had (28 against 34). Two steps of it failed. The worst case of 28 us was no bound: from the copy's start the chain took 1.3 to the gather's issue (0.6 predicted), 1.3 for the gather (2), 11.5 for the loads (11.6), 5.2 for the write (2), 7.9 for the read (8) and 3.8 on GpSimd, 31.1 in all. The write is the term that was mis-sized: from its issue to the read's it took 5.2 us behind 24 loads, at a DMA share of 0.73 (303.70 to 308.90), and 1.6 us in group 3 (363.14 to 364.75), at 0.11. And "the buffers that it frees are wanted only a group later" looked at buffers and not at the queues: GpSimd's masks for the group after stand behind the three operations, and SyncE's loads of the rows of maxima behind the read. Half of these rows, the causal ones, are wanted 22 us after they are made (299.40 to 321.40) and not 34. Rival 2 had the chain decide from 29 us on in group 3, and 1880 us with a read of twice the length. The read made twice gave 1886, but paid in the first middle group and by way of SyncE's queue (experiment 5): that the two numbers are so close is chance.

**Shared bank**: hidden, as argued (experiment 2). Of the 0.9 us taken off for group 3, the 0.3 for a copy that shows did not come (4.91 us for the two steps around it). The whole group gained 6.04 us, 6.1 were predicted.

**The ends, b = 0 to 2.** The projection at 5.7 us was right at b = 0 (5.73), with terms each off by a little: `turned_sums` 1.92 us for 1.5, `spread_sums` 2.05 for 1.8, the reciprocal 0.36 for 0.2, the copy 0.69 for 0.6 to 1.2. The step that failed is that all ends are alike: behind b = 1 and 2 the clock was low, the projection began 6.98 and 7.29 us behind the copy, and the whole stretch to the next tiles cost 1.8 us more than at b = 0. Nothing in [rows 6] could tell that. With passes of 128 columns it was gone (experiment 7), but it was gone with narrow passes too in experiments 3 and 6, so its cause is open.

**The end, b = 3.** `project` began 8.99 us behind the copy, 8.3 predicted, 9.78 before [rows 7]:

```profile
1574.74 1.65 PE L170 MATMUL PS<-wp,arena 128*128 128x256 f32 x3 [2.23 <-DVE arena L1184]
```

0.8 of the 1.5 us came, and to the end of the program even that was gone (+ 0.75). "With shorter gaps some of that may come back" was the wrong hope.

**Rival 1** did not come: VectorE has 28.22 us of work in 34.43, and TensorE waits for its maxima mainly behind the turn (1.35 and 0.58 us ahead of the weight loads at 301.39 and 302.52).

## What to carry to other kernels

When a producer waits twice per step for the same consumer, compare the two waits: a deeper ring takes away the distance between them, step after step, and that product can be trusted to a few per cent. When work is sent off through a longer way "with time enough", find what stands behind its last instruction in every queue it uses, the issuing one among them, not when its buffer is needed; here the slack was 1.9 us on GpSimd and some 8 us in SyncE's queue, and not a group. And when an experiment gives the expected number, look whether the expected wait gave it: in experiment 5 it did not. And taking work away, or doing it sooner, can cost time: look at what the freed engine will then run into.

## What the runs showed of the hardware

- GpSimd's operations on SBUF (multiplications and an addition of 128x512) hold up VectorE's work on SBUF: a cast of 16x128 took 0.84 us for 0.21, a subtraction with both inputs in SBUF 1.38 us for 0.28, while reductions from PSUM kept their 1.2 us. On a path that TensorE waits for, this cost the kernel 10.5 us (experiments 3 and 4).
- An fp32 pass with a 128-column weight load takes 0.12 us for 4 columns (1.92 us for 16) and 0.126 us for 128 (2.02 for 16).
- Behind b = 3, 16 passes of 128 columns took 2.8 to 3.8 us in nine traces in which passes of 4 columns and a standstill lay ahead, and 2.05 us in three in which passes of 128 columns and the same standstill did. Behind b = 1 the granted clock over that stretch was 0.71 in the changed kernel and 1.00 with the wide passes, but `spread_sums` took 2.05 us there with narrow ones as well in experiments 3 and 6.
- A write of 16 KB took 5.2 us from its issue to the next DMA's behind 24 loads of 64 and 128 KB, and 1.6 us without them. A read with an outer dimension of 4 had a DMA share of 0.27, one with 32 outermost, in eight DMAs, 0.40.
- The length of the same stretch between two attentions was anything from 294.3 to 301.2 us, and repeated to 0.1 us in two executions of the changed kernel (experiment 1, with 305.7 at most, has a ring of two in it). It differed between versions whose edits lie elsewhere, so gains below some 5 us are not to be judged by one stretch, and hardly by the whole kernel.
